# Cross-attention kernel: batch 0's queries and keys ahead of all values, norms in small portions, another order in the tail

## The reference

```
L0: x = attention(LN1(x), LN1(x)) + x        # self, 16 heads of 16, scale 1/8
    x = attention(LN2(x), context) + x       # cross, 77 keys
    x = geglu(LN3(x)) + x                    # 256 -> 2 x 1024 -> 256, gate * sigmoid(1.702 gate)
L1: Q, K, V from x, context, context; softmax(Q K^T / 16) V Wfc + b
    out = rms_norm(that + x, w)              # x * rsqrt(mean(x*x) + 1e-8) * w
```

## Time and profile before

| | us |
|---|---|
| median of three runs | 746.22 |
| profiled execution | 746.0 |
| its span | 743.6 |
| PE busy | 658.1 (89%) |
| DVE busy | 541.3 (73%) |
| ACT busy | 487.8 (66%) |
| POOL busy | 99.2 (13%) |

### The profile page before, as it was taken

One profiled execution on the slowest core, in us unless ns is written; L12 is line 12 of the kernel. 1 busy time (PEld: TensorE's weight loads), 2 busy tenths in 40 slices (PEclk: granted clock), 3 DMA queues, 4 the chain that ended last, 5 costly groups with the idle time before them and its releaser, 6 DMA issues.

```text
span 743.6 us, 11160 instructions
## 1 busy us (share of the span) xinstructions
PE 658.1 (89%) x4072; PEld 317.0 (43%) x4072; DVE 541.3 (73%) x929; ACT 487.8 (66%) x853; POOL 99.2 (13%) x152
## 2 busy tenths in 40 slices
PE   3989799999999999999999886778799999999981
PEld 2644122222222222222224333425458888888870
DVE  6678989999999999999993637736853944344367
ACT  3543389999999999999998662547374233332374
POOL 2071710000000000000000201345110110000004
PEclk9999699999999999999999997989999999999995
DMA  9448350202020110100000021021000000000003
GB/s 304 182 138 280 96 203 1 72 1 71 2 72 2 33 41 1 30 2 29 2 2 1 14 92 39 17 86 45 2 2 1 0 1 1 1 1 1 1 0 113
DMA packets 35113, 36.87 MB, mean 50 GB/s; under 512 B 6132, under 2 KB 28276, under 8 KB 34804
## 3 DMA queue, kind: packets, MB, share of 16 engines
q1 hardware_dynamic: 33904, 35.87, 14.7%
q0 software_dynamic: 1024, 0.24, 0.3%
q10 hardware_dynamic: 132, 0.07, 0.0%
HBM read 23.09 MB, written 12.74 MB: 48 GB/s over the span
## 4 chain that ended last, share of the span: by engine, by line
PE 63%; DVE 18%; ACT 11%; issue 5%; DMA 1%; POOL 1%; SPq 0%; ACTq 0%; DVEq 0%; POOLq 0%
PE ps L935 15%; PE ps L923 10%; DVE mm L1560 7%; PE ps L719 6%; ACT probs L1318 5%; PE ps L1121 4%; PE ps L752 4%; PE ps L1122 4%; PE ps L1123 4%; PE ps L896 3%; PE ps L705 2%; DVE tok L1538 2%; PE ps L727 2%; PE ps L1038 2%; PE ps L1137 2%
## 5 line engine op out<-in xcount | busy, mean ns | idle before, releaser
L1318 ACT ACTIVATE probs<-ps,unfit 128x512 f32<-128x512 f32 x512 | 311.3, 691 | 29.0 <-PE ps L923 24.2
L1560 DVE TENSOR_REDUCE mm<-ps 128x2 f32<-128x1024 f32 x256 | 299.5, 1220 | 13.8 <-PE ps L752 9.8
L923 PE MATMUL ps<-stack 50*128 50x512 f16 x512 | 146.9, 388 | 7.1 <-ACT probs L1318 1.2
L935 PE MATMUL ps<-probs,v 128*32 128x512 f32 x1024 | 137.3, 608 | 2.6 <-ACT outT L1323 2.6
L752 PE MATMUL ps<-stack 48*128 48x512 f16 x512 | 108.6, 391 | 12.6 <-DVE mm L1560 6.6
L923 PEld LDWEIGHTS ps<-stack 50*128 50x128 f16 x512 | 36.9, 93 | 172.4 <-ACT probs L1318 164.4
L1418 ACT ACTIVATE early<-ps,cols 128x512 f32<-128x512 f32 x32 | 22.0, 688 | 89.8 <-PE ps L1123 89.8
L1819 DVE SCALAR_TENSOR_TENSOR hid<-ps,cols,early 128x512 f32<-128x512 f32 x32 | 24.0, 750 | 72.2 <-PE ps L1123 72.2
L1373 ACT ACTIVATE probs<-ps,unfit 96x1024 f32<-96x1024 f32 x32 | 35.5, 1109 | 34.2 <-PE ps L1029 34.1
L612 POOL TENSOR_TENSOR x<-x,rows 128x512 f32<-128x512 f32 x24 | 31.9, 1340 | 150.6 <-DVE tok L1538 150.5
L1121 PE MATMUL ps<-x_hi,wff_hi 128*128 128x512 f32 x128 | 51.4, 401 | 0.0
(11 more groups left out here) (168 smaller groups left out, 868.9 us busy)
## 6 DMA issues: line engine op xcount, KB each, us to landing
v_groups<-early SPq DMA_DIRECT2D x8, 512.0 KB, 3.4
stack<-q_parts SPq DMA_DIRECT2D x64, 64.0 KB, 2.0
v<-v_groups SPq DMA_DIRECT2D x8, 512.0 KB, 4.0
x<-in_x SPq DMA_DIRECT2D x4, 512.0 KB, 7.7
q_parts<-probs SPq DMA_DIRECT2D x8, 256.0 KB, 3.8
k_parts<-probs SPq DMA_DIRECT2D x8, 256.0 KB, 2.5
stack<-k_parts SPq DMA_DIRECT2D x16, 128.0 KB, 2.5
stack<-q_parts SPq DMA_DIRECT2D x64, 32.0 KB, 1.8
```

Of the source, the lines that this page charges most:

```text
L923: eng.matmul(ps[:, st_bank(n), :], stack[rows_of(tile, KROWS), SLOTS + slot, q, P * kc:P * kc + P], qs[rows_of(tile, KROWS), slot, half, q ...
L935: mm_ = eng.matmul(ps[32 * h:32 * h + 32, PV, :], v1[:, G % 2, kc, 32 * h:32 * h + 32], probs[:, k % 2, h, :], start=(kc == 0), stop=(kc = ...
L1318: eng.activation(probs[:, k % 2, HEADS[h], :], ps[:, st_bank(n), :], ACT.Exp, scale=unfit[:, 0:1]).then_inc(exp_done, 1)
L1560: eng.tensor_reduce(dst, ps[:, 2 * slot:2 * slot + 2, :], AX.X, ALU.max).then_inc(s_red, 1)
```

## The change

It has four parts.

1. Prologue. PE, ACT and SP do all eight query and key units of batch 0 first, then its values. On PE six values follow the projections, then the transposes of block 3 and tops(1), then the last two values. On ACT four values come before the squares, two after them, and two after the copies of block 3. SP stores the eight parts, waits until they have landed, issues load_group(0), and then stores the values and loads them. On DVE the norm of block 3 follows the last remainder instead of the one before it. FIRST_PAIR becomes 0. The first maxima are transposed on PE after the two value setups, ahead of the remaining tiles.
2. tick(n) takes the number of steps: four once per piece of the chain, two in reduce_2 and attended_2.
3. SETUPS names other units for three of the first setups, and SP issues load_max_2(2) ahead of two stores.
4. Tail. PE transposes block 3 ahead of weighing block 2; ACT's order changes, and it scales block 0 only; POOL multiplies block 0 only; DVE does the last step of blocks 1, 3 and 2 in one operation a tile, with one root for blocks 2 and 3 together. SP stores 0, 1, 3, 2.

```diff
-        SETUPS = {(2, 3): 1, (3, 1): 1, (3, 3): 1, (4, 0): 1, (7, 0): 1, (7, 1): 2, (7, 2): 1, (7, 3): 1}
+        SETUPS = {(2, 2): 1, (2, 3): 2, (3, 1): 1, (7, 0): 1, (7, 1): 2, (7, 2): 1, (7, 3): 1}
-        FIRST_PAIR = 2
+        FIRST_PAIR = 0
# SP
-            for blk in range(BLOCKS):
-                if blk == 2:
-
-                    parts_stored(eng, PROJ_B0)
-                    load_group(0)
-                    v_stored(KC)
-                    load_v(0)
+            for u in range(PROJ_B0):
+                store_parts(u)
+            parts_stored(eng, PROJ_B0)
+            load_group(0)
+            for t in range(0, KC, 2):
+                store_v(t)
+            v_stored(KC)
+            load_v(0)
+            for blk in range(2, BLOCKS):
...
             load_max_2(1)
+            load_max_2(2)
             for u in range(half, half + NC):
                 store_parts(u)
-            load_max_2(2)
# PE
-                    if blk == 0 and i == 0:
-                        eng.wait_ge(tops_read, 1)
-                    values(TPB * blk + i)
                     if i == 1:
                         turn(LN1, blk + 1)
+            eng.wait_ge(tops_read, 1)
+            for t in range(KC - 2):
+                values(t)
             turn(LN1, BLOCKS - 1)
             turned(LN1, BLOCKS - 2)
             eng.wait_ge(pool_step, EARLY_SET)
             tops(1)
+            for t in range(KC - 2, KC):
+                values(t)
             turned(LN1, BLOCKS - 1)
...
+            eng.wait_ge(su_done, SETUP_1)
+            eng.wait_ge(m_step, 3)
+            eng.matmul(ps[0:96, MISC, 0:P], mpart[:, 0, :], identh[:, :], start=True, stop=True).then_inc(m_turned, 1)
             while first_scores:
                 tile_of_scores()
-                if len(first_scores) == 2 * FIRST_TILES - 18:
...
             l1_turn(2)
             l1_weigh(1)
+            l1_turn(last)
             l1_weigh(2)
-            l1_turn(last)
# ACT
                 if blk == 2:
+                    for t in range(TPB):
+                        values(t)
...
                     eng.activation(ctx_sq, ctxT[:, :, :], ACT.Square).then_inc(w_squared, 1)
+                    for t in range(TPB, KC - 2):
+                        values(t)
                     turn_copy(LN1, BLOCKS - 1)
+                    for t in range(KC - 2, KC):
+                        values(t)
...
             turn_copy(X3, last)
+            l1_squares(0)
             l1_turn_copy(2)
-            l1_squares(0)
             l1_exps(last)
+            l1_turn_copy(last)
             l1_squares(1)
-            l1_turn_copy(last)
             l1_scale(0)
             l1_squares(2)
-            l1_scale(1)
             l1_squares(last)
-            l1_scale(2)
# DVE
-                    if i == 2:
+                    if i == 2 + blk:
                         norm(0, blk + 2)
...
                     add(n, KC * b + i)
-                    tick()
                     if t > 0:
                         eng.wait_ge(y_added, TILES * n + KC * b + i)
                         stats(n + 1, blk, t - 1)
-                        tick()
...
-                    tick()
+                    tick(4)
                     yield
-                    tick()
...
+            def l1_final(blk, roots):
+                eng.wait_ge(l_root, roots)
+                for t in range(TPB):
+                    y = x[:, TPB * blk + t, :]
+                    eng.scalar_tensor_tensor(out=y, in0=y, scalar=rms[:, blk, t:t + 1],
+                                             in1=rows[:, ROW_W, :], op0=ALU.mult, op1=ALU.mult).then_inc(l_last, 1)
...
-            l1_root(0)
+            l1_root(0, 1)
             l1_residual(2)
-            l1_root(1)
             l1_residual(last)
-            l1_root(2)
-            l1_root(last)
-            eng.wait_ge(l_root, BLOCKS)
...
+            l1_root(1, 2)
+            l1_final(1, 2)
+            l1_root(2, BLOCKS)
+            l1_final(last, 3)
+            l1_final(2, 3)
```

More of the change, by code:

```diff
@@ L563, in _ @@
             out_v = a["out"].rearrange("b (t p) d -> p (b t) d", p=P)
-            for blk in range(BLOCKS):
-                if blk < BLOCKS - 1:
-                    eng.wait_ge(l_out, TPB * (blk + 1))
+            for n, blk in enumerate((0, 1, BLOCKS - 1, 2)):
+                if n == 0:
+                    eng.wait_ge(l_out, TPB)
                 else:
-                    eng.wait_ge(l_last, TPB)
+                    eng.wait_ge(l_last, TPB * n)
                 eng.dma_start(out_v[:, TPB * blk:TPB * blk + TPB, :], x[:, TPB * blk:TPB * blk + TPB, :]).then_inc(y_out, 16)
@@ L658, in _ @@
                         eng.tensor_tensor(lo, m.rearrange("p (t n) -> p t n", t=HT), hi, ALU.subtract).then_inc(m_parts, 1)
[L661 to L664, removed]
+            for i in range(TPB):
+                eng.wait_ge(l_scaled, i + 1)
+                eng.tensor_tensor(x[:, i, :], x[:, i, :], rows[:, ROW_W, :], ALU.mult).then_inc(l_out, 1)
         @block.tensor
@@ L840, in _ @@
                 tile_of_scores()
+            eng.wait_ge(su_done, SETUP_1)
+            eng.wait_ge(m_step, 3)
+            eng.matmul(ps[0:96, MISC, 0:P], mpart[:, 0, :], identh[:, :], start=True, stop=True).then_inc(m_turned, 1)
             while first_scores:
                 tile_of_scores()
-                if len(first_scores) == 2 * FIRST_TILES - 18:
-                    eng.wait_ge(su_done, SETUP_1)
-                    eng.wait_ge(m_step, 3)
-                    eng.matmul(ps[0:96, MISC, 0:P], mpart[:, 0, :], identh[:, :], start=True, stop=True).then_inc(m_turned, 1)
             eng.wait_ge(rest_done, PROJ_2)
@@ L1275, in _ @@
                     high(u)
-                    values(TPB * blk + i)
-                    if blk < 2 and i == 1:
+                    if blk >= 2:
+                        values(TPB * blk + i)
+                    elif i == 1:
                         turn_copy(LN1, blk + 1)
@@ L1492, in _, with tick @@
             under_way = [iter(())]
-            def tick():
-                for _ in range(4):
+            def tick(n):
+                for _ in range(n):
                     next(under_way[0], None)
@@ L1763, in reduce_2 @@
                                   AX.X, ALU.max).then_inc(s2_red, 1)
-                tick()
+                tick(2)
                 if m == KC // 2 - 1:
@@ L1846, in l1_residual, with l1_root @@
                                              in1=x[:, n, :], op0=ALU.mult, op1=ALU.add).then_inc(l_y, 1)
-            def l1_root(blk):
-                eng.wait_ge(l_sq, TPB * (blk + 1))
-                for _ in root_steps(ss1[:, blk, :], rms[:, blk, :], ms[:, blk, :], half_ms[:, blk, :], 1.0 / D, RMS_EPS, l_root):
-                    pass
+            def l1_root(first, end):
+                eng.wait_ge(l_sq, TPB * end)
+                for _ in root_steps(*(v[:, first:end, :] for v in (ss1, rms, ms, half_ms)), 1.0 / D, RMS_EPS, l_root):
+                    pass
+            def l1_final(blk, roots):
[4 more added lines that the diff above has]
+                                             in1=rows[:, ROW_W, :], op0=ALU.mult, op1=ALU.mult).then_inc(l_last, 1)
             last_piece, after_cross = after_cross, chain(1, 1)
@@ L1877, in _ @@
             l1_residual(1)
-            l1_root(0)
+            l1_root(0, 1)
             l1_residual(2)
-            l1_root(1)
             l1_residual(last)
-            l1_root(2)
-            l1_root(last)
-            eng.wait_ge(l_root, BLOCKS)
-            for t in range(TPB):
-                y = x[:, TPB * last + t, :]
-                eng.scalar_tensor_tensor(out=y, in0=y, scalar=rms[:, last, t:t + 1],
-                                         in1=rows[:, ROW_W, :], op0=ALU.mult, op1=ALU.mult).then_inc(l_last, 1)
+            l1_root(1, 2)
[3 more added lines that the diff above has]
+            l1_final(2, 3)
 def kernel(**inputs):
```

## The result

The changed kernel is slower. In 20 executions each its median is 755.4 us (750.5 to 761.3), that of the kernel before 749.75 (743.0 to 751.9); the ratio is 1.0091, with a 95% interval from 1.0067 to 1.0115, or +6.8 us. I had forecast -5.0. All ratios leave out executions that took over 1.5% more than the fastest of the same kernel.

A forecast was written before the change was run, and what follows sets the result against it. PE is busy nine tenths or more in most of the span, so gains lie where it stands still: prologue, self-to-cross handover, tail. Terms summed to -5.0 us, from 746.0 to 741.0; range 734.5 to 749.

The forecast's parts named there:

- prologue: Up to the first weighing matmul: value stores behind load_group(0) leave PE idle about 6 us; +6.3 us (ends +3.5, +9.5).
- last self group: First block there: PE's 1.11 us wait for an add behind the whole norm goes; -1.1 us (ends 0, -1.5).
- first block after self: After self-attention: 2.9 of a 4.48 us wait for a reduce goes, plus half the slow clock's cost; -5.0 us.
- second block after self: Late norm ends PE's transposes 1.1 us later, load_max_2(2) moves ahead of two stores; net -0.6 us (ends +1, -3).
- first block after cross: After cross-attention: 2.0 of a 3.74 us wait goes, and 1.0 of slow matmuls; -3.0 us (ends -1.5, -3.5).
- second block after cross: Norm unfinished at the feed-forward's start, PE waits some 3.1 us and may lose clock; +4.0 us (ends +1, +7.6).
- setups: Three early setups move to where PE waits for query loads, filling an idle that lowered the clock; -2.0 us.
- tail: Behind the last feed-forward matmul: two of POOL's three groups removed, one common root on DVE; -3.6 us (ends -2.5, -4.2).
- Rival B: Prologue: the store of values causes no wait, so the prologue is even; 734.7 us, chance 0.17.
- Rival C: Handover, 404 to 560 us: matmul, exponential and maxima DMA loop replaces the waits, half the gain seen; 746.9 us, chance 0.23.
- The clock: After self-attention: 9.3 us at half clock, worth up to 4.2 us if shorter idle keeps the clock up; half taken.
- Rival A: The clock eats the gain: stretches after stalls stay at half clock, shortened waits still lower it; +4.7, 750.7 us, chance 0.10.

The follow-up runs named there:

- e1: Kernel before with only the prologue's part of the change (SP, PE and ACT order, FIRST_PAIR, the maxima's turn): ratio 1.0093, +7.0 us.
- e4: Kernel before with only the earlier setups and load_max_2(2) ahead of the stores: ratio 0.9938, -4.6 us.
- e2: Kernel before with only the tail's part of the change: ratio 0.9972, -2.1 us.
- e3: Kernel before with only the norm's small portions (four steps per tile of a chain, two in reduce_2 and attended_2): ratio 1.0038, +2.8 us.
- e6: Changed kernel, but SP issues the first two stores of values ahead of the parts' wait and the first group's loads: ratio 0.9955, median 746.1 us.
- e7: Kernel before with tail, setups, small portions for first blocks (four copies held until tile 6), second blocks at once: ratio 0.9893, -8.0 us.
- e9: Changed kernel with two value stores before loads, second blocks' norms at twice the rate, later tok copies after cross-attention: ratio 0.9784, median 733.75 us.
- e11: Changed kernel with second blocks' norms at twice the rate and late copies after cross-attention, but the first kernel's whole prologue: ratio 0.9750, median 733.1 us.

## Why the prediction was wrong

The sum was -5.0 and the traces give +9.6 (+6.8 by the ratio). By the prediction's own steps, "trace" being by how much PE's matmuls behind the step stand later, after against before, and "alone" what the part's own run gave:

| step | forecast | trace | alone |
|---|---|---|---|
| prologue | +6.3 | +6.6 | +7.0 (e1) |
| last self group | -1.1 | 0 | |
| first block after self | -5.0 | -3.6 | |
| second block after self | -0.6 | +2.0 | |
| first block after cross | -3.0 | +2.1 | |
| second block after cross | +4.0 | +6.2 | |
| setups | -2.0 | +0.2 | -4.6 (e4) |
| tail | -3.6 | -3.9 | -2.1 (e2) |

The five rows of the norm's portions, from the last self group on, sum to -5.7 in the forecast (its -0.6 counts the move of load_max_2(2) too). Alone (e3) they are +2.8 us, a mean over executions. Of the 11.8 us between the forecast and the ratio this is 8.5, by far the largest part. The waits named below repeat in e3's trace; what the trace column holds of the clock is one pair of executions.

**Prologue: right, with its mechanism.** Its steps are in the trace: projection 5 behind a remainder at 28.11 (forecast 29), PE's wait of 5.73 us (forecast 6.3), the copy behind the store's landing, the first score tile at 54.03 (54), L847 at 87.19 (87.6), the weighing at 97.65 (98.5). e6 shows that the store's place in SP's list is the cause. Rival B falls.

**Last self group: a misreading.** I took the first pair's norm to be split. The condition `if n == b: finish_norm()` finishes it at once for chain(0, 0), and the row at 418.92 is the old one with its 1.11 us.

**First block after cross-attention: the failed step, 5.1 us of the traces' miss.** I wrote "wait of 3.74, of which 2.0 goes". 2.8 went, and 3.58 us came in front of the next thing that PE takes from DVE, with the slow clock behind it (0.50 for 5.7 us): +2.1 instead of -3.0. I followed the norm's steps to the reduction that they released and no further, though I had listed what is late next for the second blocks. Rival C had the mechanism (the waits are replaced) but named the wrong loop: DVE's own order, not the chain over the exponential and the transfer. e7 and e9 show it: the four copies put elsewhere, and 0.98 + 0.88 are left.

**Second blocks: right in kind, too small, 4.8 us.** The late norm at the feed-forward's start stood in the forecast with 3.1 us of wait; it was 2.17 + 0.80. Its slow clock came to 3.2 us, where I had 0.9. For the block after self-attention I gave the late norm 1.1 us and let the setups pay for it; the trace has 2.16 + 0.94 of wait, where 1.33 had been, and the clock at 0.65 behind it.

**Setups: right alone in sign, not to be read from the two traces.** My -2.0 is small against -4.6. The +0.2 is no price of theirs: it is +1.0 of slow clock behind 490 us, less 0.8 at a wait of 0.90 us that the kernel before has at 549.56; e3, without the setups, lacks that wait too, and e4 keeps it.

**The clock was the term that I sized from one execution.** The forecast let shortened waits leave the clock up ("half" of 4.2 us). In this trace it fell after 1.32 us as well, 7.1 us at 0.52, and PE's matmuls in the first block after self-attention came down by 0.8 us, not 2.1. Over the whole stage the waits gave back 1.7 us and the matmuls took 8.6 more.

The Trainium skill (TensorE: Matmul & The Clock Gate, "What's actually happening") says that the number of matmuls that run cold at a kernel's start differs from run to run of the same kernel. The runs here agree: the first projection took 3.75 us in the kernel before and 1.96 in e11, with the same instructions ahead of it. They show it for later stretches too: the same order and the same long waits (4.48 and 3.75 us among them) took 153.7 us in one execution and 163.8 in e2's, at 0.93 and 0.85. The trace before, from which I took the earlier trace rows, was one of the quick ones, and I took the clock's price from it alone.

Rival A, which had the right sign (750.7 us forecast, chance 0.10), came nearest: +4.7 against +6.8. It priced the clock at every stall but not the replaced waits.

What stays open: why the quickest executions of the kernel before keep the clock up at the same waits, and so how much of the +2.8 us of the portions is their new waits and how much the clock behind them.

## What to carry to other kernels

Work on a full engine is not removed by cutting it into portions; it is moved, and the gain of the place it leaves is real only when the next two or three things that others take from that engine are followed too (as shipped +2.8 us, the same steps placed by that rule -6.6). A store that frees a staging slot belongs ahead of loads that are wanted later, whatever its data is for. Where TensorE waits some microseconds, count the slow clock after it as a cost of its own, and compare it over many executions, not two traces.

## What the runs showed of the hardware

Spare matmuls inside a 4.5 and a 3.7 us wait made the kernel 5.0 us faster, though what TensorE waits for comes no earlier: with them the granted clock around both was 1.00, and none of the six executions took over 747.1 us. The clock fell behind a wait as short as 1.32 us (461.5 us, 0.52), but behind the same wait in e11 it stayed at 1.00 (452 to 459 us). The same instruction order with the same long waits took 153.7 and 163.8 us in two executions, the idle time 27.6 and 26.6. Over 29 executions of the kernel before the time spread from 743.1 to 753.1 us, the mean granted clock with it from 0.965 to 0.949.
